# Multiplying forty quads of the first stage in fp32r halves, rounded by ScalarE, with the rests made by GpSimd

## The chip, the cores and the metric

The kernel runs on one core of one Trainium2 chip. The metric is the device time of one execution in microseconds: the median of three runs. Beside it stands one execution taken by the hardware profiler, from which all times of instructions come.

## The reference

The function takes x (8192 x 128) and a sparse but densely stored matrix A (8192 x 8192, some 256 MB in fp32) with positive entries and a full diagonal:

```
def lap_mul(A, x):
    d = 1 / sqrt(sum(A, axis=-1))
    return d[:, None] * (A @ (d[:, None] * x))
z  = leaky_relu(lap_mul(A, x) @ W1 + b1, 0.1)
d2 = sq[:, None] + sq[None, :] - 2 z @ z.T          # sq = sum(z*z, -1)
S  = exp(-sqrt(max(d2, 0) + 1e-10) / 2)             # only the 4 largest of a row are kept
out = lap_mul(S + A, x) @ W2 + b2
return layernorm(x + out)
```

For this case the first `lap_mul` matters: the sums of A's rows, x scaled by them (`xs`), and the product of A with `xs`.

## The kernel before

A is stored transposed and cut into 16 x 16 blocks of 512 x 512. A block, called a quad, is one load of 1 MB onto 128 partitions x 2048 fp32 numbers (four tiles of 128 x 512). Quad (b, q) belongs to row block b and column block q.

The **first stage** streams all 256 quads once, row block by row block (`one`, loaded by SyncE, SP, at L673). VectorE adds the quads of a row block (`add_quad`, L1489, 15 adds, then `add_tiles`, L1494 and L1495), TensorE sums the result over the partitions (`row_sums`, L782, with a column of ones), VectorE copies the sums (`read_sums`, L1499), ScalarE takes a square root (L1052), and VectorE refines its reciprocal and scales x (`scale_xs`, L1507), which gives `xs` for column block b. As soon as `xs` of column block q is there, quad (b, q) can be multiplied while it still lies in its slot: `product` (L773), four fp32 products of 128x128 by 128x512 that accumulate in the PSUM bank of row b. A profile shows each fp32 product as two records, so a quad has eight. Row block b multiplies its quads with q < b when they arrive, and (b, b) after its own scaling, early in the next row; 158 of the 256 quads are multiplied here. When a row block is closed, ScalarE saves its bank (L1063).

A quad lies in one of 18 slots of 1 MB: in `ring`, in `cache` (the place of zh and zl of a later stage) and in parts of R1 and R2. `plan_ab` fixes the order of loads and products, and `next_slot` fixes the slot of each load from the estimate `left` of when a quad is done with. SP waits before a load until the quad that held the slot is added and, if it is multiplied here, multiplied.

Each engine works through its own list in program order. VectorE's list for row b is: the first add (which needs two quads), `read_sums(b - 1)`, the second add, `scale_xs(b - 1)`, the remaining adds, `add_tiles(b)`. TensorE's list is the products of the row, then `row_sums`.

The **second stage** loads the other 98 quads again (`two`) and multiplies them in fp32r halves: ScalarE rounds a quad to fp32r (`round_2`, L1045, two buffers `ah`), VectorE subtracts to get the rest (`rest_2`, L1572, `al`), and TensorE makes three products for each tile: high xs by high quad (L836), low xs by high quad (L837), high xs by rest (L840), twelve in all. The halves of `xs` are made near the end of the first stage, in the last row block: high ones by ScalarE (`high_half`, L1037), low ones by VectorE (`low_half`, L1513).

Behind that come the scores and the search for the four nearest (TensorE, ScalarE, VectorE's MAX8 and FIND_INDEX8), during which GpSimd makes rests for a third pass over A (`rest_of_piece`, L1305), and a tail, in which GpSimd makes two rests of whole quads (L1448) and VectorE the others. GpSimd does nothing in the first stage; its first work are casts of 128x128 (L1278, L1279) in the second.

Of the kernel before, what the change touches and what calls it, by code (L numbers as in the profile page):

```python
# [6 lines left out]
F32 = mybir.dt.float32  # L7
# [8 lines left out]
BC = 512  # L16
# [11 lines left out]
SLOTS_END = (0, 1, 2, 3, SLOTS_2, SLOTS_2 + B // TB)  # L28
# [4 lines left out]
YB = 7  # L33
SUMS_EARLY = 2
STEP_2 = 3
LOW_AT = 10
# [50 lines left out]
def plan_ab():  # L87

    loads, products, closed = [], [], {}
    for b in range(B):  # L90
        keep = [q for q in range(b + 1, B) if b in held(q)]
        low = list(range(b))
        high = [q for q in range(b + 1, B) if q not in keep]
        order = []
        while low or high:
            more_high = len(high) * (len(order) + 1) > 0 and len(high) >= len(low)
            order.append((high if more_high else low).pop(0))
        order += keep[::-1] + [b]
# [31 lines left out]
def build(nc, x, at, W1, b1, W2, b2, consts, out, xs_dram, xh_dram, xl_dram, acc_dram):  # L130
# [7 lines left out]
    closed = {b: max(prod_at[bq] for bq in flat if bq[0] == b) for b in range(B)}  # L138


    def left(n):
        b, q = one[n]
        if (b, q) not in prod_at:
            return n + 2
        return n + 3 if q < b else B * (q + 1) + AHEAD + 4

    n_slots = SLOTS_A + SLOTS_X + len(SLOTS_Y)
# [14 lines left out]
    for n in range(n_one + len(two)):  # L162
        if n < n_one - STREAM_END:
            k = next_slot(n, [*range(SLOTS_A), *(k for k, b in SLOTS_Y.items() if left(n) <= B * (b + 1)),
                              *(k for k, b in X_FROM.items() if left(n) <= B * b)])
# [13 lines left out]
    with ctx:  # L179
# [44 lines left out]
        slots_a += [R2[:, b * BC:b * BC + SLOT].rearrange("p (k c) -> p k c", c=BC) for b in SLOTS_Y.values()]  # L224
        total = R1[:, N + 2 * SLOT:N + 3 * SLOT]
# [119 lines left out]
        xl_ok = sem("xl_ok")  # L345
        rnd_2 = sem("rnd_2")
# [105 lines left out]
        halves = range(min(q for r, q in two), B)  # L452
# [200 lines left out]
        def _(sp):  # L653
# [8 lines left out]
            for n, (b, q) in enumerate(one + two):  # L662
                m = before_of[n]
                if m is not None and m >= n_one:
                    sp.wait_ge(al_ok, m - n_one + 1)
                elif n >= n_one and slot_of[n] in X_FROM:
                    sp.wait_ge(prod1, len(flat))
                    sp.wait_ge(xl_ok, len(halves))
                elif m is not None:
# [90 lines left out]
        def _(pe):  # L760
# [3 lines left out]
            def product(b, q):  # L764
                n = load_at[b, q]
                first = started[b] == 0
                started[b] += 1
                pe.wait_ge(ld_a[slot_of[n]], turn_of[n])
                pe.wait_ge(xs_ok, q + 1)
                if first and b >= YB:  # L770
                    pe.wait_ge(y_saved, b - YB + 1)
                for k in range(TB):
                    i = pe.matmul(PS[:, b % YB], xs[:, q * TB + k], slots_a[slot_of[n]][:, k],  # L773
                                  start=first and k == 0, stop=prod_at[b, q] == closed[b] and k == TB - 1)
# [51 lines left out]
            for n, (b, q) in enumerate(two):  # L826
# [6 lines left out]
                pe.wait_ge(xl_ok, q - halves[0] + 1)  # L833
# [194 lines left out]
        def _(act):  # L1028
# [10 lines left out]
            def round_2(n):  # L1039
                act.wait_ge(ld_a[slot_of[n_one + n]], turn_of[n_one + n])  # L1040
                if n < 2:
                    free_of_stage_1(act, SLOTS_B + n)
                else:
                    act.wait_ge(prod2, n - 1)
                act.activation(ah_2[n % 2][:, :, :], slots_a[slot_of[n_one + n]], ACT.Copy).then_inc(rnd_2, 1)  # L1045

            for b in range(B):
                if b == B - 1:
                    for q in halves[:-2]:
                        high_half(q)  # L1050
                act.wait_ge(sums_read, b + 1)
                act.activation(tiny[:, 0, 0:TB], rowsum[:, b * TB:(b + 1) * TB], ACT.Sqrt).then_inc(root_ok, 1)  # L1052
                if b == B - 1:
# [3 lines left out]
                    round_2(1)  # L1057
                while saved < B and all(q <= b for r, q in flat if r == saved):
# [6 lines left out]
                    saved += 1  # L1065
                if b < B - 1:
# [205 lines left out]
        def _(pool):  # L1272
# [161 lines left out]

            pool.wait_ge(z2_ok, 2 + GT // TB)
# [35 lines left out]
        def _(v):  # L1471
# [44 lines left out]
            for b in range(B):  # L1516
                for i in range(1, B):
# [5 lines left out]
                    if b == B - 1:  # L1523
                        for k, q in enumerate(halves[:-2]):
                            if i == LOW_AT + k // 2:
                                low_half(q)
                add_tiles(b)

            read_sums(B - 1)
# [36 lines left out]
            def rest_2(n):  # L1566
                v.wait_ge(rnd_2, n + 1)
                if n < 2:
                    v.wait_ge(prod1, max(prod_at[r, q] for r, q in flat if q // TB == n))
# [210 lines left out]
```

## Time and profile before

| | us |
|---|---|
| median of 3 runs | 2683.36 |
| lowest and highest run | 2681.94, 2683.89 |
| profiled execution, its time | 2679.84 |
| profiled execution, span from first to last instruction | 2678.0 |
| TensorE busy | 2456.8 |
| VectorE busy | 2319.3 |
| ScalarE busy | 1606.8 |
| GpSimd busy | 1193.2 |
| first stage: last row sums on TensorE at | 708.07 |
| second stage: first product at | 718.86 |

The span has stages with different limits, so the totals say little about the first one. The profile can be cut into stretches, with the busy time of each engine in each; there a full stretch of TensorE is one in which every microsecond saved or added on TensorE counts. The order in time of one engine gives the price of one instruction and the idle time ahead of it, with what ended it.

### The profile page before, as it was taken

To read this page: it belongs to the slowest core of one execution; us is meant where nothing else is said; L and a number is where in the kernel's file an instruction comes from. 1 tells how busy PE (TensorE), PEld (TensorE's weight loads), DVE (VectorE), ACT (ScalarE), POOL (GpSimd) and SP (SyncE) were. 2 spreads that over 40 slices of the span, in tenths; PEclk is the share of its full clock that TensorE was granted. 3 is DMA by queue.
4 is the path that set the end of the run, shared out by engine and by line. 5 is a ranking of instruction groups with operands and counts; after the bars stand their busy time and mean duration, and the time that the engine had idled before them with its cause. 6 is when DMAs were issued, how large, how long until landed. Compare 5 with 4: busy or idle time off the path is not lost.

```text
span 2678.0 us, 29073 instructions
## 1 busy us (share of the span) xinstructions
PE 2456.8 (92%) x9356; PEld 1710.4 (64%) x9356; DVE 2319.3 (87%) x1411; ACT 1606.8 (60%) x1905; POOL 1193.2 (45%) x987
## 2 busy tenths in 40 slices
PE   0467999999999999899999999999999998899998
PEld 0133444444577777577778787877878775577776
DVE  7998889976788887999999999989999877488887
ACT  0000000000377776899998989889898876477776
POOL 0000000000000000067788888878787895777772
PEclk9678999999999999999999999999999999999999
DMA  9999999997699981035565555545555568999996
GB/s 383 421 405 402 399 421 421 421 421 291 236 374 345 341 329 52 0 114 170 147 170 147 168 149 141 175 135 177 146 173 148 168 179 320 398 400 402 400 402 244
DMA packets 147948, 718.58 MB, mean 268 GB/s; under 512 B 19024, under 2 KB 26960, under 8 KB 86608
## 3 DMA queue, kind: packets, MB, share of 16 engines
q1 hardware_dynamic: 124384, 670.49, 66.7%
q0 software_dynamic: 18800, 37.77, 5.7%
q10 hardware_dynamic: 4608, 8.39, 0.8%
q8 instruction: 79, 1.29, 0.2%
q14 instruction: 77, 0.63, 0.1%
HBM read 680.40 MB, written 36.18 MB: 268 GB/s over the span
## 4 chain that ended last, share of the span: by engine, by line
PE 59%; DMA 9%; issue 9%; DVE 9%; ACT 9%; POOL 3%; SPq 0%; ACTq 0%; POOLq 0%; DVEq 0%
PE PS L773 19%; PE PS L872 5%; PE PS L874 5%; PE PS L873 5%; DMA ring<-at 4%; ACT R L1147 3%; PE PS L840 3%; DMA R<-at 3%; PE PS L916 3%; PE PS L917 3%; PE PS L927 3%; PE PS L836 2%; PE PS L837 2%; PE PS L977 2%; DVE R L1629 2%
## 5 line engine op out<-in xcount | busy, mean ns | idle before, releaser
L1305 POOL TENSOR_TENSOR al<-ring,ah 128x1024 fp32r<-128x1024 f32 x264 | 643.7, 2439 | 181.6 <-ACT ah L1118 168.0
L1629 DVE MAX8 R<-R 128x8 f32<-128x8192 f32 x64 | 555.8, 8685 | 68.6 <-ACT R L1147 68.4
L1147 ACT ACTIVATE R<-PS 128x1024 f32<-128x1024 f32 x512 | 518.0, 1018 | 112.0 <-PE PS L880 82.6
L1632 DVE FIND_INDEX8 R<-R,R 128x8 uint32<-128x8192 f32 x64 | 555.9, 8685 | 0.3 <-issue 0.3
L1278 POOL CAST zst<-zh 128x128 fp32r<-128x128 f32 (+1 forms) x64 | 26.3, 411 | 1112.8 <-DVE zl L1564 811.1
L872 PE MATMUL PS<-zh,zst 128*128 128x512 f32 x1024 | 407.2, 398 | 28.5 <-ACT PS L1133 12.7
L874 PE MATMUL PS<-zh,zst 128*128 128x512 f32 x1024 | 400.4, 391 | 0.0
L873 PE MATMUL PS<-zl,zst 128*128 128x512 f32 x1024 | 400.2, 391 | 0.0
L1133 ACT ACTIVATE PS<-R 128x1024 f32<-128x1024 f32 x310 | 318.0, 1026 | 6.6
L1052 ACT ACTIVATE tiny<-rowsum 128x4 f32<-128x4 f32 x16 | 3.3, 205 | 482.1 <-DVE rowsum L1499 482.1
L773 PE MATMUL PS<-cache,R 128*128 128x512 f32 x584 | 263.5, 603 | 16.7 <-DMA cache<-at 11.3
L1489 DVE TENSOR_TENSOR R<-R,cache 128x2048 f32<-128x2048 f32 x106 | 242.9, 2292 | 19.8 <-DMA cache<-at 17.5
L872 PEld LDWEIGHTS PS<-zh,zst 128*128 128x128 f32 x1024 | 192.2, 188 | 96.9 <-ACT PS L1133 25.0
L1464 POOL DMA_INDIRECT R<-xs_dram,R x176 | 192.5, 1094 | 61.4 <-issue 52.7
L874 PEld LDWEIGHTS PS<-zh,zst 128*128 128x128 f32 x1024 | 192.3, 188 | 41.6
L873 PEld LDWEIGHTS PS<-zl,zst 128*128 128x128 f32 x1024 | 192.3, 188 | 39.8 <-issue 0.7
L773 PEld LDWEIGHTS PS<-cache,R 128*128 128x128 f32 x584 | 112.3, 194 | 157.6 <-issue 144.7
L773 PE MATMUL PS<-ring,R 128*128 128x512 f32 x384 | 175.9, 605 | 11.9 <-DMA ring<-at 6.4
L1572 DVE TENSOR_TENSOR al<-ring,ah 128x2048 fp32r<-128x2048 f32 x66 | 151.0, 2290 | 35.5 <-ACT ah L1045 33.0
L1489 DVE TENSOR_TENSOR R<-R,ring 128x2048 f32<-128x2048 f32 x72 | 165.0, 2291 | 11.6 <-DMA ring<-at 9.6
L987 PE MATMUL PS<-ah_t,xsh 128*128 128x512 f32 x368 | 153.3, 417 | 11.8 <-ACT ah_t L1197 11.6
L1045 ACT ACTIVATE ah<-ring 128x2048 fp32r<-128x2048 f32 x66 | 126.4, 1915 | 62.7 <-PE PS L840 59.9
(181 smaller groups left out, 4515.5 us busy)
## 6 DMA issues: line engine op xcount, KB each, us to landing
R<-at SPq DMA_DIRECT2D x160, 1024.0 KB, 14.7
ring<-at SPq DMA_DIRECT2D x148, 1024.0 KB, 9.4
ring<-at SPq DMA_DIRECT2D x264, 512.0 KB, 3.8
cache<-at SPq DMA_DIRECT2D x117, 1024.0 KB, 20.3
acc_dram<-R POOLq DMA_DIRECT2D x78, 256.0 KB, 5.7
raw_sq<-at SPq DMA_DIRECT2D x18, 1024.0 KB, 14.4
raw_z<-at SPq DMA_DIRECT2D x18, 1024.0 KB, 15.3
raw_ring<-at SPq DMA_DIRECT2D x17, 1024.0 KB
```

The source lines that it names most:

```text
L773: i = pe.matmul(PS[:, b % YB], xs[:, q * TB + k], slots_a[slot_of[n]][:, k], start=first and k == 0, stop=prod_at[b, q] == closed[b] and k ...
L872: pe.matmul(bank, zst[:, par, 0], zh[:, cols], start=not on_seed, stop=False, skip_group_check=True)
L873: pe.matmul(bank, zst[:, par, 0], zl[:, cols], start=False, stop=False, skip_group_check=True)
L874: i = pe.matmul(bank, zst[:, par, 1], zh[:, cols], start=False, stop=on_seed, skip_group_check=True)
L987: pe.matmul(bank, xsh[:, t], ah_t[n % HIGH_T][:, k], start=from_zero and k == 0, stop=False, skip_group_check=True)
L1133: act.activation(pair(False, 0, c), sq_row[c], ACT.Copy).then_inc(seeded, 1)
L1147: act.activation(score[j % 2][:, c * EC:(c + 1) * EC].rearrange("p (b c) -> p b c", b=2), pair(first, j, c), ACT.Copy).then_inc(copied, 1)
L1305: pool.tensor_tensor(al[:, k % SPLIT], raw[k % RAW], ah[:, k % SPLIT].bitcast(F32), ALU.subtract)\
L1464: pool.indirect_dma_start(gx[f % GX][:, j, m], None, xs_dram, bass.IndirectOffsetOnAxis(ap=sidx[:, FIN[f] * TB + j, m:m + 1], axis=0))\
L1489: v.tensor_tensor(total.rearrange("p (k c) -> p k c", c=BC), other, slots_a[slot_of[n]], ALU.add)\
L1629: v.max(top[:, j], score[j % 2]).then_inc(dve3, 1)
L1632: v.max_index(place[:, j], top[:, j], score[j % 2]).then_inc(placed, 1)
```

## The change

In row blocks 11 to 15 (`SPLIT_FROM`) the quads of column blocks 0 to 7 (`SPLIT_Q`), forty in all, are no longer multiplied as fp32. ScalarE rounds such a quad into one of the two `ah` buffers (`round_1`), GpSimd writes the rest, the raw quad less the rounded one, over the raw quad (`rest_1`), after VectorE has added it, and TensorE makes the twelve fp32r products. The other quads of these rows stay as they are. The order of loads in these rows now alternates between split and plain quads. The halves of `xs` for columns 0 to 7 are made earlier, in row block 10, the high ones by ScalarE (`early_high`) and the low ones by GpSimd (`early_low`). The slots change with that: the `ah` buffers and the early halves lie where slots were, these are not used any more from row 10 or 11 on, and two new ones (`SLOTS_W`) lie over `xs` of columns 0 to 7, which nobody reads in fp32 after row 10. VectorE's low halves of the other columns move behind all adds of the last row.

```
+SPLIT_FROM, SPLIT_Q = 11, 2 * TB
+SOON = 3
...
+        if b >= SPLIT_FROM:
+            plain_q = [q for q in range(SPLIT_Q, B) if q != b]
+            order = [q for both in zip(range(SPLIT_Q), plain_q) for q in both]
+            order += range(len(plain_q), SPLIT_Q)
...
-        halves = range(min(q for r, q in two), B)
+        halves = range(SPLIT_Q, B)
...
+                if (b, q) in split_at:
+                    m = split_at[b, q]
+                    bank = PS[:, b % YB]
+                    pe.wait_ge(xl_early, q + 1)
+                    pe.wait_ge(rnd_1, m + 1)
+                    for k in range(TB):
+                        pe.matmul(bank, half_of_xs(0, q)[:, k], ah_2[m % 2][:, k], start=first and k == 0, stop=False,
+                                  skip_group_check=True)
+                        pe.matmul(bank, half_of_xs(1, q)[:, k], ah_2[m % 2][:, k], start=False, stop=False,
+                                  skip_group_check=True)
+                    pe.wait_ge(low_1, m + 1)
+                    for k in range(TB):
+                        i = pe.matmul(bank, half_of_xs(0, q)[:, k], low_of_slot[slot_of[n]][:, k], start=False,
+                                      stop=False, skip_group_check=True)
+                    i.then_inc(prod1, 1)
+                    return
...
+            def round_1(m):
+                n = load_at[split1[m]]
+                act.wait_ge(ld_a[slot_of[n]], turn_of[n])
+                if m < 2:
+                    free_of_stage_1(act, SLOTS_B + m)
+                else:
+                    act.wait_ge(prod1, prod_at[split1[m - 2]])
+                act.activation(ah_2[m % 2][:, :, :], slots_a[slot_of[n]], ACT.Copy).then_inc(rnd_1, 1)
+
             for b in range(B):
-                if b == B - 1:
-                    for q in halves[:-2]:
-                        high_half(q)
+                if b == SPLIT_FROM - 1:
+                    for q in range(SPLIT_Q):
+                        early_high(q)
                 act.wait_ge(sums_read, b + 1)
                 act.activation(tiny[:, 0, 0:TB], rowsum[:, b * TB:(b + 1) * TB], ACT.Sqrt).then_inc(root_ok, 1)
...
+                row_split = [m for m, (r, q) in enumerate(split1) if r == b + 1]
+                for m in row_split[:SOON]:
+                    round_1(m)
...
+                for i, m in enumerate(row_split[SOON:]):
+                    round_1(m)
...
+            def rest_1(m):
+                n = load_at[split1[m]]
+                pool.wait_ge(rows_added, (B - 1) * (n // B) + max(n % B, 1))
+                hold(pool)
+                pool.wait_ge(rnd_1, m + 1)
+                hold(pool)
+                pool.tensor_tensor(low_of_slot[slot_of[n]][:, :, :], slots_a[slot_of[n]],
+                                   ah_2[m % 2][:, :, :].bitcast(F32), ALU.subtract).then_inc(low_1, 1)
+
+            for q in range(SPLIT_Q):
+                early_low(q)
+            for m in range(len(split1)):
+                rest_1(m)
...
+            for q in halves[:-2]:
+                low_half(q)
             read_sums(B - 1)
             scale_xs(B - 1)
```

On ScalarE, at the end of the first stage, the list of before has a square root for each row block (R_50 is R2, where a closed bank is saved), and then the high halves and the first roundings of the second stage:

```order
L1052 ACTIVATE tiny<-rowsum 128x4
L1063 ACTIVATE R_50<-PS 128x512
L1037 ACTIVATE xsh<-R_49 128x512 x9
L1052 ACTIVATE tiny<-rowsum 128x4
L1045 ACTIVATE ah_81<-ring 128x2048
```

Between two square roots now stand eight roundings; this is the beginning of row block 12, where `ah_91` and `ah_92` are the two buffers:

```order
L1119 ACTIVATE tiny<-rowsum 128x4
L1112 ACTIVATE ah_91<-R_49 128x2048
L1112 ACTIVATE ah_92<-R_49 128x2048
L1112 ACTIVATE ah_91<-cache 128x2048
L1133 ACTIVATE R_50<-PS 128x512
L1112 ACTIVATE ah_92<-cache 128x2048
```

Three roundings of the next row stand behind the square root, then the save of the closed bank, then the other five. On TensorE, row block 12 of before begins behind the row sums of row 11 with plain fp32 products, four a quad:

```order
L782 MATMUL PS<-ones,R_49 128x1 x4
L773 MATMUL PS<-ring,R_49 128x512 x4
L773 MATMUL PS<-R_49 128x512 x4
L773 MATMUL PS<-cache,R_49 128x512 x20
L773 MATMUL PS<-ring,R_49 128x512 x4
```

Now the first quad is a split one, from the last pair of its products with the rounded half on; `low_80` is the rest that GpSimd has written over the slot:

```order
L811 MATMUL PS<-ah_91,xsh 128x512
L813 MATMUL PS<-ah_91,xsl 128x512
L817 MATMUL PS<-low_80,xsh 128x512 x4
L824 MATMUL PS<-ring,R_49 128x512 x4
L811 MATMUL PS<-ah_92,xsh 128x512
L813 MATMUL PS<-ah_92,xsl 128x512
```

Four products with the rest (L817) stand between the products with the rounded half (L811, L813) and the next plain quad (L824), so TensorE passes them only when GpSimd is done with that quad.

## Rows read from the trace of the kernel before

**Rows 1.** Busy time by stretch, row blocks 10 to 15: length, then engines, clock, DMA.

```profile
core 0: us, PE busy (x) PEld busy (x) DVE busy (x) ACT busy (x) POOL busy (x), PEclk, DMA share, GB/s
432.29:470.95 38.66, 38.66 (x99) 17.61 (x98) 36.37 (x24) 0.80 (x2) 0.00 (x0) 1.00 1.01 421
470.95:513.04 42.09, 42.09 (x106) 19.13 (x106) 39.08 (x25) 0.80 (x2) 0.00 (x0) 1.00 1.01 420
513.04:558.57 45.53, 45.53 (x115) 20.66 (x114) 37.73 (x24) 0.80 (x2) 0.00 (x0) 1.00 1.02 421
558.57:607.53 48.96, 48.96 (x123) 22.17 (x122) 37.64 (x24) 0.80 (x2) 0.00 (x0) 1.00 1.01 421
607.53:659.92 52.39, 52.39 (x130) 23.69 (x130) 37.63 (x24) 0.80 (x2) 0.00 (x0) 1.00 0.84 327
659.92:718.86 58.94, 58.94 (x146) 26.65 (x146) 48.05 (x43) 10.43 (x16) 0.00 (x0) 1.00 0.54 192
```

**Rows 2.** TensorE in order of time: start, length, line, operands, count.

```profile
603.28 3.60 PE L773 MATMUL PS<-R 128*128 128x512 f32 x8
606.72 0.95 PE L782 MATMUL PS<-ones,R 128*128 128x1 f32 x8
...
722.00 0.39 PE L836 MATMUL PS<-ah,xsh 128*128 128x512 f32 x1
...
723.81 1.07 PE L840 MATMUL PS<-al,xsh 128*128 128x512 f32 x4
724.72 0.39 PE L836 MATMUL PS<-ah,xsh 128*128 128x512 f32 x1
```

**Rows 3.** SP's waits from 400 to 760: us in total, times, longest.

```profile
SPq L672 <- PE PS L773: 201.6, 57, 13.8
```

**Rows 4.** VectorE in order of time, rows 14 and 15, idle time in brackets.

```profile
607.70 0.16 DVE L1499 COPY rowsum<-PS 128x4 f32<-128x4 f32 x1 [10.56 <-PE PS L782]
...
687.82 1.29 DVE L1513 TENSOR_TENSOR xsl<-R,xsh 128x512 fp32r<-128x512 f32 x2
...
709.06 0.16 DVE L1499 COPY rowsum<-PS 128x4 f32<-128x4 f32 x1 [1.86 <-PE PS L782]
...
710.68 0.69 DVE L1507 TENSOR_TENSOR R<-R,dsc 128x512 f32<-128x512 f32 x1
```

**Rows 5.** GpSimd's subtractions: ns min/median/max of a line; one in time.

```profile
L1448 POOL TENSOR_TENSOR al_t<-R,ah_t x2: 4562/4565/4568, 2243.7 to 2248.2; 128x2048 fp32r<-128x2048 f32 x2
...
L1305 POOL TENSOR_TENSOR al<-ring,ah x264: 2373/2410/2700, 1146.4 to 2235.7; 128x1024 fp32r<-128x1024 f32 x132
...
1142.33 1.30 POOL L1389 TENSOR_TENSOR xgl<-R,xgh 128x512 fp32r<-128x512 f32 x1
```

**Rows 6.** ScalarE in order of time: a square root; a rounding of the second stage.

```profile
607.96 0.21 ACT L1052 ACTIVATE tiny<-rowsum 128x4 f32<-128x4 f32 x1 [31.34 <-DVE rowsum L1499]
...
731.42 1.92 ACT L1045 ACTIVATE ah<-ring 128x2048 fp32r<-128x2048 f32 x1 [1.65 <-DMA ring<-at]
```

**Rows 7.** VectorE, then GpSimd, in order of time, 811 to 817 us.

```profile
811.32 2.29 DVE L1572 TENSOR_TENSOR al<-R,ah 128x2048 fp32r<-128x2048 f32 x1
814.07 2.31 DVE L1572 TENSOR_TENSOR al<-R,ah 128x2048 fp32r<-128x2048 f32 x1 [0.46 <-ACT ah L1045]
...
811.53 2.23 POOL L1278 CAST zst<-zh 128x128 fp32r<-128x128 f32 x1 [811.08 <-DVE zl L1564]
813.72 0.28 POOL L1279 CAST zst<-zl 128x128 fp32r<-128x128 f32 x1
813.95 0.29 POOL L1278 CAST zst<-zh 128x128 fp32r<-128x128 f32 x1
814.19 2.35 POOL L1279 CAST zst<-zl 128x128 fp32r<-128x128 f32 x1
```

**Rows 8.** The page's group of VectorE's search: busy, mean ns, idle before.

```profile
L1629 DVE MAX8 R<-R 128x8 f32<-128x8192 f32 x64 | 555.8, 8685 | 68.6 <-ACT R L1147 68.4
```

**Rows 9.** TensorE early in the first stage, with the idle time ahead.

```profile
119.66 3.70 PE L773 MATMUL PS<-ring,R 128*128 128x512 f32 x8 [1.94 <-DMA ring<-at]
...
269.15 5.32 PE L773 MATMUL PS<-ring,R 128*128 128x512 f32 x8 [4.50 <-DMA ring<-at]
```

More of the change, by code:

```diff
@@ L97, in plan_ab @@
             order.append((high if more_high else low).pop(0))
+        if b >= SPLIT_FROM:
+            plain_q = [q for q in range(SPLIT_Q, B) if q != b]
+            order = [q for both in zip(range(SPLIT_Q), plain_q) for q in both]
+            order += range(len(plain_q), SPLIT_Q)
+            assert not keep
         order += keep[::-1] + [b]
@@ L138, in build @@
     closed = {b: max(prod_at[bq] for bq in flat if bq[0] == b) for b in range(B)}
+    split1 = [(b, q) for b in range(SPLIT_FROM, B) for q in loads[b] if q < SPLIT_Q]
+    assert split1 == sorted(split1, key=lambda bq: prod_at[bq])
+    split_at = {bq: m for m, bq in enumerate(split1)}
     def left(n):
@@ L163, in build @@
         if n < n_one - STREAM_END:
-            k = next_slot(n, [*range(SLOTS_A), *(k for k, b in SLOTS_Y.items() if left(n) <= B * (b + 1)),
+            k = next_slot(n, [*(k for k in range(SLOTS_A)
+                                if k not in SLOTS_SPLIT or left(n) <= B * SLOTS_SPLIT[k] + TB),
+                              *(k for k in SLOTS_W if n >= B * SPLIT_FROM + TB),
+                              *(k for k, b in SLOTS_Y.items() if left(n) <= B * (b + 1)),
                               *(k for k, b in X_FROM.items() if left(n) <= B * b)])
@@ L224, in build @@
         slots_a += [R2[:, b * BC:b * BC + SLOT].rearrange("p (k c) -> p k c", c=BC) for b in SLOTS_Y.values()]
+        slots_a += [R1[:, k * SLOT:(k + 1) * SLOT].rearrange("p (k c) -> p k c", c=BC) for k in range(len(SLOTS_W))]
+        slot_top = [top_of["ring"] + k * SLOT * 4 for k in range(SLOTS_B)]
+        slot_top += [top_of["R1"] + (N + k * SLOT) * 4 for k in range(2)]
+        slot_top += [top_of["zh"] + k * SLOT * 4 for k in range(SLOTS_A - SLOTS_2)]
+        slot_top += [top_of["R1"] + k * SLOT * 4 for k in (2, 3)]
+        slot_top += [top_of["R2"] + b * BC * 4 for b in SLOTS_Y.values()]
+        slot_top += [top_of["R1"] + k * SLOT * 4 for k in range(len(SLOTS_W))]
+        low_of_slot = {k: sb(f"low_{k}", [P, TB, BC], F32R, at=slot_top[k])
+                       for k in sorted({slot_of[load_at[bq]] for bq in split1})}
         total = R1[:, N + 2 * SLOT:N + 3 * SLOT]
@@ L451, in build @@
         ends = list(itertools.accumulate(sum(r == b for r, q in two) for b in blocks2))
-        halves = range(min(q for r, q in two), B)
+        assert min(q for r, q in two) < SPLIT_Q
+        halves = range(SPLIT_Q, B)
         last_quad = {}
@@ L668, in _ @@
                     sp.wait_ge(xl_ok, len(halves))
+                elif m is None and slot_of[n] in SLOTS_W:
+                    k = SLOTS_W.index(slot_of[n])
+                    sp.wait_ge(xl_early, (k + 1) * TB)
+                    sp.wait_ge(prod1, max(prod_at[r, q] for r, q in flat if r < SPLIT_FROM and q // TB == k))
                 elif m is not None:
@@ L767, in product @@
                 started[b] += 1
+                if first and b >= YB:
+                    pe.wait_ge(y_saved, b - YB + 1)
+                if (b, q) in split_at:
+                    m = split_at[b, q]
[13 more added lines that the diff above has]
+                    return
                 pe.wait_ge(ld_a[slot_of[n]], turn_of[n])
                 pe.wait_ge(xs_ok, q + 1)
-                if first and b >= YB:
-                    pe.wait_ge(y_saved, b - YB + 1)
                 for k in range(TB):
                     i = pe.matmul(PS[:, b % YB], xs[:, q * TB + k], slots_a[slot_of[n]][:, k],
-                                  start=first and k == 0, stop=prod_at[b, q] == closed[b] and k == TB - 1)
+                                  start=first and k == 0, stop=prod_at[b, q] == closed[b] and k == TB - 1,
+                                  skip_group_check=b >= SPLIT_FROM)
                 i.then_inc(prod1, 1)
@@ L832, in _ @@
                     pe.wait_ge(y_ok, blocks2.index(row_of_bank[b]) + 1)
-                pe.wait_ge(xl_ok, q - halves[0] + 1)
+                if q in halves:
+                    pe.wait_ge(xl_ok, q - halves[0] + 1)
                 pe.wait_ge(rnd_2, n + 1)
@@ L1065, in _ @@
                     saved += 1
+                for i, m in enumerate(row_split[SOON:]):
+                    round_1(m)
+                    if b == B - 2 and i >= 1:
+                        for q in halves[2 * (i - 1):min(2 * i, len(halves) - 2)]:
+                            high_half(q)
                 if b < B - 1:
@@ L1568, in rest_2 @@
                 if n < 2:
-                    v.wait_ge(prod1, max(prod_at[r, q] for r, q in flat if q // TB == n))
+                    free_of_stage_1(v, SLOTS_W[n])
                 else:
```

30 lines of the change are left out of this document (22 added, 8 removed).

## The prediction

> **What bounds the kernel now.** I read the busy time by stretches first, cut at the ends of the row sums of successive row blocks. In row blocks 10 to 15 TensorE is busy for the whole of every stretch at the full granted clock, GpSimd is not used at all, ScalarE hardly, and VectorE is busy for 37.6 to 37.7 us in each of rows 12 to 14, whatever the row's length [rows 1]. So the row lengths, 42.09, 45.53, 48.96, 52.39 and 58.94 us for rows 11 to 15, are TensorE's. Its order in time gives the prices: one fp32 quad takes 606.72 - 603.28 = 3.44 us, the four row-sum products 607.53 - 606.72 = 0.81 us, and one quad of the second stage, which is already multiplied in fp32r halves, 724.72 - 722.00 = 2.72 us, of which the last four products, those of the rest, are 724.72 - 723.81 = 0.91 and the first eight 1.81 [rows 2]. That nothing else limits these rows shows on SP's queue: it waited 201.6 us for products that hold slots [rows 3]. A microsecond won or lost here moves everything behind it, since TensorE goes straight from this stage into the next.
>
> VectorE has a second role. Its first add of a row runs early, but before the second it waits for the row sums of the row before (10.56 us at 607.70) [rows 4]; so of a row's adds all but the first lie between two row sums, and 37.6 us is what such a row costs it.
>
> **The change, part by part.**
>
> TensorE. Forty quads (8 in each of rows 11 to 15) go from 3.44 to 2.72 us: 40 x 0.72 = 28.8 us removed, all of it on the path. This is the gain that everything else is set against.
>
> GpSimd. Forty rests of 128x2048 are new. The trace has two passes of exactly this shape, 4.565 us each, and the half-size ones at 2.41 agree [rows 5]. That is 8 x 4.565 = 36.5 us a row, on an engine that was idle. Eight low halves of xs (128x512, 1.30 us each [rows 5]) are added in row 10.
>
> ScalarE. Forty roundings of 1.92 us [rows 6], 15.4 us a row: cheap, but their place matters. ScalarE rounds the first quad of row b+1 only after its square root of row b, which starts 607.96 - 607.53 = 0.43 us after TensorE has ended the row sums [rows 1, 6]. TensorE's next product is that quad. So it waits 0.43 + some 0.1 + 1.92 + some 0.15 for the hand-over = 2.6 us, does its first eight products until 4.4, and waits again for GpSimd's rest, which can begin at 2.6 and is there at 2.6 + 4.57 + 0.15 = 7.3: 2.9 us more. Each row begins with 5.5 us of waiting where there was none. Queued behind TensorE's wait are all products of the row, so no other work covers it. Two rounding buffers also mean that quad m is rounded only when quad m-2 is multiplied, so GpSimd never gets more than about one quad ahead.
>
> The end of a row. Where a plain product lies between two split ones, the pair takes 3.44 + 2.72 = 6.2 us and GpSimd's 4.57 fits. Behind the last plain one the split quads follow one another at GpSimd's pace, 1.85 us slower than TensorE's. Following quad by quad with these prices gives waits of 6.8 us in row 11 (1.4 + 3 x 1.8), 4.2 in row 12, 2.4 in row 13 and none in rows 14 and 15.
>
> Without any further cost the rows then change by -8 x 0.72 + 5.5 + tail: +6.5, +3.9, +2.1, -0.3, -0.3, together +12 us, and about 1 us more where the last loads wait for slots that split quads hold longer. The saving is eaten by the rows' beginnings and ends alone.
>
> VectorE beside GpSimd. The change lets GpSimd read two SBUF operands while VectorE adds two SBUF operands, which the first stage never did before. The trace has two encounters of this kind. VectorE's subtraction of two SBUF tiles ran from 811.32 to 813.61; a GpSimd cast that started inside it, at 811.53, took 2.23 us and ended at 813.76. The next two casts fell in VectorE's gap and took 0.28 and 0.29. The fourth started at 814.19 inside VectorE's next subtraction (814.07 to 816.38) and took 2.35 [rows 7]. A cast of 0.28 us that lasts until 0.15 us behind VectorE's end was held off for the whole instruction. Against MAX8, with one SBUF input, GpSimd's passes run at 2.41 us [rows 5, 8]. So the two share something that a two-input instruction of VectorE keeps to itself. What no row shows is the other direction, a GpSimd pass of 4.57 us that starts first. Bounds: nothing (both overlap, +12 us as above) or full serial work. I take full serial work, because the encounters in rows 7 are the nearest there are, both of them, and GpSimd's gain from being stopped would be the same sum anyway: if GpSimd is stopped for each add, its 36.5 us still have to be found between 37.6 us of VectorE.
>
> The Trainium skill, in "SBUF — State Buffer", section "Who interferes with whom", says that a VectorE instruction with two SBUF inputs contends with a GpSimd instruction that reads SBUF, and that whichever starts first keeps the shared pair for its whole length. The casts of rows 7 agree for the side that the trace shows. By this rule the sum is the serial one; without it, the +12 us above.
>
> The sum. A row on the shared resource: 37.6 + 36.5 = 74.1 us; up to 16 hand-overs of 0.15 add 2.4; I take 76. Adds, rests and products of a row cannot slide into another row, since adds wait for row sums, row sums for all products of the row, and those for the last rest. Rows 11 to 14: 4 x 76 - (42.09 + 45.53 + 48.96 + 52.39) = +115.0. Row 15: 76 less the 2.3 of a next row's first add, then on VectorE the low halves, now all behind the adds (six at 0.645 = 3.9 us), then 711.37 - 709.06 = 2.3 until xs is scaled [rows 4], then the last product, 3.44: 83.3 against 58.94, +24.4. Row 10: VectorE has 36.4 of 38.66 us to do [rows 1] and eight passes of 1.30 are put among them: 46.8, +8.1. Together +147.5 us. The profiled execution took 2679.84 us; 2827.3. The median of the runs shown is 3.5 us above it: **2831**. The next stages keep their length: their loads, roundings and rests are the same, and GpSimd is done by then.
>
> **The rivals.**
>
> A, no sharing loss (the two long casts had another cause): +13 us, 2697. For: each of the four engines has time. Against: rows 7, where two casts of four on the same line differ by eight times and only by what VectorE ran.
>
> B, faster: GpSimd's pass is short and nothing contends. The mechanism is the wait at the rows' beginnings and ends, which shrinks with the pass. At VectorE's 2.29 us the beginning costs 2.6 + 0.6, the tail nothing, and a row is worth -5.8 + 3.2 = -2.6: -13 us, 2670. It decides at about 3.6 us per pass, where the waits equal 28.8. Against: 4.565 us twice in [rows 5]. ScalarE's late start remains in any case.
>
> C, GpSimd holds the shared resource for half of its pass: a row is 37.6 + 18.3 and hand-overs, 57: rows 11 to 14 +39, row 15 +5, row 10 +3: +47, 2731. No row speaks for or against.
>
> D, VectorE wins every encounter as long as it has an add queued: GpSimd's first rest then starts at about 37.6, the first quad ends at 43, and the remaining 41 us of the row follow as in the case without contention: 84 a row, 8.4 more than the forecast in each of five, 2873. Rows 7 don't decide it, since VectorE had gaps there. To this side belongs TensorE's clock: after an idle time of 1.94 us eight products took 3.70, but after 4.50 us 5.32 [rows 9]; the new waits lie between and beyond. TensorE then has slack in most of the row, so I count a few microseconds at most.
>
> **How the numbers follow.** Forecast 0.62, C 0.12, A 0.13, D 0.07, B 0.06. Forecast, C and D hold 0.81, so the range goes from C's side, 2715, to just beyond D, 2880. About 0.2% is what a measurement can tell from no change here, 5.4 us. A is 13 us slower, with an uncertainty of about as much, so a sixth of it ends faster and a sixth within 0.2%. Faster: 0.06 + 0.02 = 0.08. Same: 0.02 from A and as much from B, 0.04. Slower: 0.88.
>
> **What would show it.** Right: GpSimd's passes in rows 11 to 15 well above 4.57 us, or VectorE's adds well above 2.29, in sum some 30 us a row; row sums 76 us apart; TensorE waiting for the rests in every row, its granted clock below 1 in places; and the second stage as long as before. Wrong: passes at 4.57 beside adds at 2.29, rows of 48 to 52 us and waits at the rows' beginnings alone (A), or rows shorter than before (B).

## The result and the profile after

The changed kernel takes 2816.7 us (median of 4 runs, 2816.41 to 2817.93) against 2682.69 before (median of 4): a ratio of 1.05, 95% interval 1.0483 to 1.0517. It is slower by 134 us; the forecast was 2831 and slower. The profiled execution took 2816.41 us, its span is 2814.6.

The stretches of after, cut at the ends of the row sums of successive row blocks as in [rows 1], are these (length, busy time of each engine with its count, granted clock of TensorE, DMA share, GB/s); the five lines are row blocks 11 to 15:

```profile
core 0: us, PE busy (x) PEld busy (x) DVE busy (x) ACT busy (x) POOL busy (x), PEclk, DMA share, GB/s
476.84:549.02 72.18, 50.03 (x137) 32.43 (x138) 71.42 (x25) 15.78 (x10) 47.63 (x8) 0.78 0.75 297
549.02:621.24 72.22, 50.52 (x145) 31.73 (x146) 71.46 (x25) 15.77 (x10) 47.29 (x8) 0.81 0.58 218
621.24:693.52 72.28, 51.88 (x153) 32.07 (x154) 71.52 (x25) 15.77 (x10) 47.73 (x8) 0.85 0.61 236
693.52:765.76 72.24, 57.42 (x161) 34.41 (x162) 71.48 (x25) 15.77 (x10) 47.71 (x8) 0.83 0.57 222
765.76:850.14 84.38, 64.06 (x181) 37.61 (x182) 79.37 (x40) 21.93 (x20) 47.74 (x8) 0.83 0.39 147
```

Three things are to be seen against [rows 1]. The full engine is now VectorE (71.5 of 72.2 us), not TensorE. A row's length no longer depends on how many quads it multiplies: four rows of 72.2 us where there were 42.09 to 52.39. And VectorE's count is the same 25 or so instructions as before, in 71.5 instead of 37.6 us, so it does the same work and is held 33.8 us a row. Rows 11 to 14 are together 288.92 - 188.97 = 99.95 us longer, row 15 84.38 - 58.94 = 25.4, row 10 44.80 - 38.66 = 6.1: 131.5 us. The second stage's first product moved by just that, from 718.86 to 850.14, and that stage itself is as long as before: from the first of its rest products to the last are 290.6 us, before 290.5. The other 5 us between the two profiled spans (2814.6 and 2678.0) lie behind it, spread over the later stages.

Where VectorE is held shows in the order in time, first VectorE, then GpSimd, from the middle of row block 12 (start, length, line, operands, count, idle time ahead in brackets):

```profile
576.43 2.29 DVE L1585 TENSOR_TENSOR R<-R,R 128x2048 f32<-128x2048 f32 x1
578.75 6.52 DVE L1585 TENSOR_TENSOR R<-R,cache 128x2048 f32<-128x2048 f32 x1
...
577.05 6.08 POOL L1524 TENSOR_TENSOR low<-cache,ah 128x2048 fp32r<-128x2048 f32 x1 [2.81 <-DVE R L1585]
```

GpSimd's pass starts at 577.05, inside VectorE's add, waits for that add's end at 578.72 and ends at 583.13, 4.41 us behind it. VectorE's next add starts at 578.75 and ends at 585.27, 2.14 us after the pass is over, so all but some 0.15 of its 2.29 us lie behind the pass. From 578.72 to 585.27 are 6.55 us for one pass and one add, which alone take 4.565 [rows 5] and 2.29 [rows 7]: 6.86. The two engines alternate, with 0.3 us of overlap at the ends. The add after the held one runs free, the next one is held by the next pass, and so on. GpSimd's 40 passes, by the slot that they read (ns: least, median, most; first and last start):

```profile
L1524 POOL TENSOR_TENSOR low<-ring,ah x17: 4544/6439/6467, 485.0 to 820.0; 128x2048 fp32r<-128x2048 f32 x17
L1524 POOL TENSOR_TENSOR low<-cache,ah x14: 4547/6405/6467, 480.5 to 769.4; 128x2048 fp32r<-128x2048 f32 x14
L1524 POOL TENSOR_TENSOR low<-R,ah x9: 4548/6430/6475, 495.6 to 828.9; 128x2048 fp32r<-128x2048 f32 x9
```

Medians of 6.4 us are one pass plus the wait for the add in progress; the least, 4.55, is the price alone. Even an instruction of four numbers is held if it has two SBUF inputs. The two operations of the Newton step on the reciprocal of row 11's sums, at the start of row 12, took 0.16 us each before; now they read:

```profile
552.74 4.46 DVE L469 TENSOR_TENSOR tiny<-tiny 128x4 f32<-128x4 f32 x1
557.24 4.48 DVE L470 TENSOR_TENSOR tiny<-tiny,rowsum 128x4 f32<-128x4 f32 x1
...
552.64 9.06 POOL L1524 TENSOR_TENSOR low<-R,ah 128x2048 fp32r<-128x2048 f32 x2 [6.36 <-DVE R L1585]
```

TensorE's list, which had no wait in these rows, now waits for the rests, for the row sums' last add and for the first rounding of a row (us in total, times, longest), and GpSimd itself mostly for VectorE's adds:

```profile
POOL low L1524 <- DVE R L1585: 116.7, 34, 6.4
PE PS L817 <- POOL low L1524: 77.1, 32, 5.8
PE PS L834 <- DVE R L1591: 15.4, 2, 9.4
PE PS L811 <- ACT ah L1112: 12.9, 5, 2.6
```

The first quad behind the row sums of row 12 answers to [rows 2]; the products with the rounded quad stand 0.43 us apart, not 0.23, until the clock is back:

```profile
620.43 1.81 PE L834 MATMUL PS<-ones,R 128*128 128x1 f32 x8
624.83 0.76 PE L811 MATMUL PS<-ah,xsh 128*128 128x512 f32 x1 [2.59 <-ACT ah L1112]
625.39 0.63 PE L813 MATMUL PS<-ah,xsl 128*128 128x512 f32 x1
625.82 0.63 PE L811 MATMUL PS<-ah,xsh 128*128 128x512 f32 x1
...
629.48 1.21 PE L817 MATMUL PS<-low,xsh 128*128 128x512 f32 x4 [1.20 <-POOL low L1524]
```

### The profile page after: what moved, and what is told of

It is laid out like the page before. It is cut to its first block, busy times and chain, and to the rows that moved or that the text cites. A ratio compares the mean times of both kernels' runs of the same rounds, so it can differ in the third digit from the quotient of the medians.

```text
span 2814.6 us, 29616 instructions
## 1 busy us (share of the span) xinstructions
PE 2490.7 (88%) x9516; PEld 1771.2 (63%) x9516; DVE 2494.0 (89%) x1408; ACT 1683.8 (60%) x1950; POOL 1462.3 (52%) x1035
## 4 chain that ended last, share of the span: by engine, by line
PE 46%; DVE 22%; ACT 9%; issue 9%; DMA 9%; POOL 4%; SPq 0%; ACTq 0%; POOLq 0%; DVEq 0%
DVE R L1585 12%; PE PS L824 8%; PE PS L925 5%; PE PS L927 5%; PE PS L926 5%; DMA ring<-at 4%; ACT R L1222 4%; DMA R<-at 3%; PE PS L969 3%; PE PS L893 3%; PE PS L980 3%; PE PS L970 3%; PE PS L889 2%; PE PS L890 2%; PE PS L1030 2%
## 5 line engine op out<-in xcount | busy, mean ns | idle before, releaser
L1585 DVE TENSOR_TENSOR R<-R,cache 128x2048 f32<-128x2048 f32 x91 | 249.3, 2740 | 16.9 <-DMA cache<-at 14.9
L1515 POOL TENSOR_TENSOR xsl<-R,xsh 128x512 fp32r<-128x512 f32 x8 | 24.4, 3086 | 450.6 <-ACT xsh L1103 450.6
L1585 DVE TENSOR_TENSOR R<-R,ring 128x2048 f32<-128x2048 f32 x80 | 235.8, 2947 | 6.5 <-DMA ring<-at 4.3
L927 PEld LDWEIGHTS PS<-zh,zst 128*128 128x128 f32 x1024 | 192.8, 188 | 41.8
L824 PE MATMUL PS<-cache,R 128*128 128x512 f32 x352 | 161.7, 610 | 17.3 <-DMA cache<-at 11.9
L1769 DVE TENSOR_TENSOR al_t<-R,ah_t 128x1024 fp32r<-128x1024 f32 x102 | 120.3, 1221 | 48.3 <-ACT ah_t L1272 48.2
```

Source lines behind the costliest of these rows:

```text
L927: i = pe.matmul(bank, zst[:, par, 1], zh[:, cols], start=False, stop=on_seed, skip_group_check=True)
L1585: v.tensor_tensor(total.rearrange("p (k c) -> p k c", c=BC), other, slots_a[slot_of[n]], ALU.add)\
```

## The experiments

The theory is the prediction's: a GpSimd pass that reads two SBUF operands and a VectorE instruction that does the same run one after the other, and a row is their sum. The rivals are that the rests are slow by themselves and TensorE waits for them whatever VectorE does, that GpSimd's writes or its memory traffic as such slow VectorE, and that the fine cut of the work is at fault. Eleven kernels tell these apart; each was timed beside runs of the kernel before (medians 2681.48 to 2684.61).

### VectorE with one input, the passes as they are

```
+if b >= SPLIT_FROM and i > 1:
+    v.max(tiny[:, 4], slots_a[slot_of[n]]).then_inc(rows_added, 1)
+    return
+if b >= SPLIT_FROM:
+    other = total.rearrange("p (k c) -> p k c", c=BC)
```

> The changed kernel, but in row blocks 11 to 15 VectorE's adds from the second on are replaced by a search of the eight largest numbers over the same quad: one SBUF input of 128x2048 where the add has two, and nearly the same length. It leaves out those adds, so the row sums of these rows are not A's; everything else, every wait too, is as in the changed kernel. Theory (a two-input instruction of VectorE and a reading pass of GpSimd keep each other out): GpSimd's rests fall from a median of 6.4 us to 4.55 beside VectorE's one-input instructions, the rows from 72.2 us to what the waits at their beginnings and ends give: 48.8, 49.5, 51.1, 52.2 us for rows 11 to 14; with 6 us from row 10, about +19 us against before, 2702 us. Rival (GpSimd's passes are slow beside other traffic, or the handshakes cost the time): rests stay above 6 us, rows near 72, time near 2817.

Measured: 2720.2 us, ratio 1.0142 (1.0122 to 1.0163), so 96.5 us of the 134 vanish although GpSimd does the same forty passes. Its passes are back at their own price (least, median, most in ns):

```profile
L1524 POOL TENSOR_TENSOR low<-ring,ah x17: 4523/4567/5532, 487.5 to 731.1; 128x2048 fp32r<-128x2048 f32 x17
```

VectorE's searches beside them from 480 to 700 us (busy, mean ns, idle before), and rows 11 and 12 as stretches:

```profile
L1586 DVE MAX8 tiny<-ring 128x8 f32<-128x2048 f32 x21 | 48.2, 2295 | 0.6
```

```profile
479.90:531.77 51.87, 41.90 (x139) 27.07 (x139) 51.10 (x25) 15.79 (x10) 37.28 (x8) 0.89 0.96 391
531.77:582.99 51.22, 44.13 (x146) 28.55 (x145) 50.46 (x25) 15.78 (x10) 37.35 (x8) 0.90 0.80 322
```

Passes of 4.567 us and searches of 2.295 us run beside each other as if alone. Rows 13 and 14 took 52.0 and 52.8. The total was put at 2702 and missed by 18 us: rows 11 to 14 are 3.1, 1.7, 0.9 and 0.6 us longer than written down, and row 15, for which nothing was counted, 10.6 us longer than before. VectorE is full here too, 51.1 of 51.87 us, and the reason is the few instructions that still have two inputs; in order of time, VectorE and then GpSimd:

```profile
535.06 4.48 DVE L469 TENSOR_TENSOR tiny<-tiny 128x4 f32<-128x4 f32 x1
539.57 4.47 DVE L470 TENSOR_TENSOR tiny<-tiny,rowsum 128x4 f32<-128x4 f32 x1
...
534.97 9.05 POOL L1524 TENSOR_TENSOR low<-R,ah 128x2048 fp32r<-128x2048 f32 x2 [5.10 <-DVE tiny L1586]
```

Two operations on four numbers cost 8.6 us of a row. They also settle what the search leaves open: it has one input less than an add, but it writes only eight numbers too. These operations write next to nothing and are held all the same, so a second input is enough. This run, too, does not show the rows free of the conflict.

### GpSimd that only writes, or reads once

```
-pool.tensor_tensor(low_of_slot[..], slots_a[..], ah_2[m % 2][..].bitcast(F32), ALU.subtract)
+pool.memset(low_of_slot[..].bitcast(F32), 0.0)          # e2_write_only
+pool.tensor_copy(low_of_slot[..], ah_2[m % 2][..].bitcast(F32))   # e7_one_read
```

> The changed kernel, but GpSimd fills the slot with zeros instead of subtracting: it writes the same 128x2048 numbers and reads nothing. It leaves out the rests. Theory (what is shared is a way of reading): VectorE's adds stay at 2.29 us, GpSimd's fills are all of one short length, and a row changes by 8 x 0.72 us less and a wait of some 2.6 us for the first rounding more, about -3 us each; with +6 from row 10 about 2674 us. Rival (the two engines keep each other out whatever GpSimd does): adds are lengthened by a fill's length eight times a row, and rows 11 to 13 grow with it.

> The changed kernel, but GpSimd copies the rounded quad over the slot instead of subtracting: one SBUF input instead of two. It leaves out the rests. A copy of 128x1024 took 1.05 us in the trace of before, so 2.1 us is the estimate for one of 128x2048. Theory (any reading pass counts): eight times a row VectorE is held up for nearly the length of a copy, a row of VectorE is 37.6 + 8 x 1.9 = 53 us, rows 11 to 14 about 53 each, +23 us, row 15 some +8, row 10 +6: about 2720 us. Rival (only two-input passes of GpSimd collide): adds at 2.29 us, rows as in the write-only run, about 2674 us.

Measured: filling 2689.56 us, ratio 1.003 (1.0019 to 1.0042); copying 2714.51, 1.0121 (1.0101 to 1.0141). First the fills and the copies (least, median, most in ns), then a group of adds beside the fills and one beside the copies, both from 480 to 700 us (busy, mean ns, idle before):

```profile
L1524 POOL MEMSET low<- x40: 1804/1811/1822, 481.0 to 708.0; 128x2048 f32 x40
```

```profile
L1524 POOL CAST low<-ah x40: 1889/3490/3951, 481.1 to 729.9; 128x2048 fp32r<-128x2048 f32 x40
```

```profile
L1584 DVE TENSOR_TENSOR R<-R,ring 128x2048 f32<-128x2048 f32 x29 | 66.5, 2292 | 9.7 <-DMA ring<-at 9.0
```

```profile
L1584 DVE TENSOR_TENSOR R<-R,ring 128x2048 f32<-128x2048 f32 x25 | 71.4, 2857 | 0.7
```

The fills are all alike within 1% and the adds stay at 2.292 us: what GpSimd writes does not collide with a two-input add. A pass with one input already does: the copies are stretched from 1.89 us to a median of 3.49 and the adds to 2.857, and rows 11 to 13 are 51.0 us each. VectorE is busy for 50.3 of them against 37.7, so each copy of 1.89 us holds it for some 1.6. The conflict is about reading, and its price goes with the length of the GpSimd pass: a shorter one holds VectorE for less. The copies came within 6 us of the 2720 written down. The fills missed their 2674 by 15.6 us; their rows (41.8, 44.1, 47.5 and 51.0 us for rows 11 to 14) are those of the next run, which shows why. (Fills did hold one instruction, which is told at the end.)

### No rests at all

```
-pe.wait_ge(low_1, m + 1)
-    i = pe.matmul(bank, half_of_xs(0, q)[:, k], low_of_slot[slot_of[n]][:, k], start=False,
+    i = pe.matmul(bank, half_of_xs(0, q)[:, k], ah_2[m % 2][:, k], start=False,
...
-for m in range(len(split1)):
-    rest_1(m)
```

> The changed kernel without GpSimd's forty rests: TensorE multiplies the rounded quad a third time in the rest's place, and waits for no rest. It leaves out the rests; ScalarE's roundings, the slots and GpSimd's eight early low halves stay. This is the most that the change could give with the rests for nothing. Theory: the saving of 0.72 us per quad is there, and each row still begins with a wait of 2.6 us for the first rounding: 5 x (-5.8 + 2.6) = -16, row 10 +6: about 2673 us. Rival (the slots or the loads limit the last rows, or ScalarE's roundings do): rows 11 to 15 not shorter than before, 2690 us or more.

Measured: 2689.46 us, ratio 1.0029 (1.0016 to 1.0041). This run missed too, by 16 us: with rests that cost nothing the kernel should have won, and it still loses 7.8 us. Rows 11 to 14 became 41.58, 44.07, 47.50 and 50.97 us, 0.5 less than before in row 11 and some 1.4 in each of the others, where 8 x 0.72 less the 2.6 us start are 3.2. The start of row 12 shows the rest of it:

```profile
517.66 0.95 PE L833 MATMUL PS<-ones,R 128*128 128x1 f32 x8
521.05 0.51 PE L811 MATMUL PS<-ah,xsh 128*128 128x512 f32 x1 [2.44 <-ACT ah L1111]
521.36 0.62 PE L813 MATMUL PS<-ah,xsl 128*128 128x512 f32 x1
521.78 0.63 PE L811 MATMUL PS<-ah,xsh 128*128 128x512 f32 x1
...
524.34 1.29 PE L816 MATMUL PS<-ah,xsh 128*128 128x512 f32 x4
525.47 3.59 PE L823 MATMUL PS<-ring,R 128*128 128x512 f32 x8
```

and the row as one stretch:

```profile
518.47:562.54 44.07, 41.63 (x146) 27.71 (x145) 37.74 (x24) 15.78 (x10) 0.00 (x0) 0.96 0.99 396
```

After the row sums and an idle time of 2.44 us the products stand 0.425 us apart from the second on (521.36 to 521.78), the pace of 1.2 GHz, against 0.227 in the second stage [rows 2]: this first quad takes 525.47 - 521.05 = 4.42 us instead of 2.72, and the granted clock of the row is 0.96. Here a wait of 2.4 us costs 4.1. On top come row 10, 6.1 us longer, and row 15, 3.5 us longer, in which VectorE waited 8.3 us for a late load.

### The plain quad first

The run before with one edit more: each pair begins with its plain quad, so that ScalarE's rounding runs under 3.44 us of products.

```
-order = [q for both in zip(range(SPLIT_Q), plain_q) for q in both]
+order = [q for both in zip(plain_q, range(SPLIT_Q)) for q in both]
```

> The run without rests, with one edit: in rows 11 to 15 the pairs of loads and products begin with the plain quad, so that TensorE has 3.44 us of work while ScalarE makes the first rounding. It leaves out the rests, as that run does. Theory (a row loses 2.5 us to the wait for the first rounding and 1.7 us more because the nine or so products behind the wait run at the lower clock): no wait and no slow products at the rows' beginnings; rows 12 to 14 another 4.2 us shorter, 39.9, 43.3, 46.8 us, row 11 held by VectorE's 37.7 at about 38.5; in sum some 15 to 19 us less than the run without rests, 2672 us. Rival (the loads or VectorE limit these rows once the rests are gone): less than 8 us gained.

Measured: 2670.18 us, ratio 0.9953 (0.9936 to 0.997), some 19 us less than without the edit. TensorE waits for no rounding, and rows 12 to 14 have the lengths written down, 39.9, 43.3 and 46.8 (row 11 took 40.3, not 38.5), with TensorE full at the full clock:

```profile
516.40:556.27 39.87, 39.87 (x146) 26.50 (x146) 37.73 (x24) 15.79 (x10) 0.00 (x0) 1.00 1.01 421
556.27:599.59 43.32, 43.32 (x154) 28.02 (x154) 37.73 (x24) 15.86 (x10) 0.00 (x0) 1.00 1.01 417
599.59:646.36 46.77, 46.77 (x163) 29.55 (x162) 37.74 (x24) 15.76 (x10) 0.00 (x0) 1.00 0.94 380
```

Each is 5.6 to 5.7 us below [rows 1], the 8 x 0.72 of the sum. In these rows the start wait with its clock was the whole difference, 4.2 us each.

### The same passes in halves, fewer rows

```
+for ks in (slice(0, TB // 2), slice(TB // 2, TB)):                # e5_half_passes
+    i = pool.tensor_tensor(low_of_slot[..][:, ks], slots_a[..][:, ks], ah_2[m % 2][:, ks].bitcast(F32), ALU.subtract)
...
-SPLIT_FROM, SPLIT_Q = 11, 2 * TB                                  # e6_from_13
+SPLIT_FROM, SPLIT_Q = 13, 2 * TB
```

> The changed kernel with each rest cut into two GpSimd passes of 128x1024. Theory (the sum counts): VectorE is held up twice as often for half as long, a row stays at 72 us within 2, the time within 10 us of 2817. Rival (it is the length of one GpSimd instruction that hurts, because a waiting short instruction of VectorE sits behind all of it): rows fall by 5 us or more.

> The changed kernel with rows 13 to 15 split instead of rows 11 to 15. Theory: a split row takes 72.2 us whatever its number, since VectorE's and GpSimd's work in it is the same: row 13 +23, row 14 +20, row 15 +25; the early halves now fall into row 12, where VectorE has 8 us to spare, and cost nothing: +68 us, 2750 us. Rival (cost in proportion to the quads, 134 x 24 / 40): +80 us, 2763 us.

Measured: halves 2813.06 us, 1.0489 (1.047 to 1.0508); from row 13 on 2751.67, 1.026 (1.0241 to 1.0279). With halves the two engines take turns in smaller steps; VectorE, then GpSimd:

```profile
572.93 4.32 DVE L1587 TENSOR_TENSOR R<-R,R 128x2048 f32<-128x2048 f32 x1
577.28 4.33 DVE L1587 TENSOR_TENSOR R<-R,cache 128x2048 f32<-128x2048 f32 x1
...
570.71 21.86 POOL L1525 TENSOR_TENSOR low<-cache,ah 128x1024 fp32r<-128x1024 f32 x5
```

Now every add is held for half a pass instead of every second one for a whole pass, 4.3 and 4.3 in place of 2.29 and 6.52, and rows are 71.4 to 72.1 us long. The sum counts, not the cut. From row 13 on, rows 13 to 15 to their sums take 71.49, 72.30 and 72.26 us while rows 11 and 12 are as before (42.09, 45.53): 68 us to the start of the second stage, which grows with the number of rows and says that the cost belongs to each row by itself. Row 12 there also makes the eight early low halves and is not longer, since VectorE has 45.53 - 37.7 = 7.8 us to spare in it, where row 10 has 2.3 [rows 1].

### The rests by VectorE

```
-for m in range(len(split1)):      # GpSimd's list
-    rest_1(m)
...
+if b >= SPLIT_FROM and i % 2 == 1 and i > 1:      # VectorE's, behind its adds; the last one behind the tiles
+    rest_1(SPLIT_Q * (b - SPLIT_FROM) + i // 2 - 1)
```

> The changed kernel with its forty rests made by VectorE, each behind the add of the quad after it, and none by GpSimd. Theory (rests and adds are one sum, whoever makes the rests, and VectorE's 2.29 us per rest is cheaper than the 4.23 us for which GpSimd holds it up): a row of VectorE is 37.6 + 8 x 2.29 = 56 us; rows 11 to 14 +35 us, row 15 about +6, row 10 +6: +47 us, 2730 us. Rival (the order and the waits of the split quads cost the rows, not the sum): rows stay near 72 us, or fall to the 42 to 51 us of the run without rests.

Measured: 2752.65 us, ratio 1.0264 (1.0245 to 1.0283). If the two engines cannot read at once, the engine that needs 2.28 us for a rest should do it, not the one that holds the other for 4.2; this is 64 us better than the change. Rows 11 to 14 take 57.1, 55.9, 57.0 and 55.5 us, as written down (56). The total was forecast 23 us lower and missed for the most part in row 15, which takes 71.9 to its sums; there VectorE waited for loads, SP's queue for products that hold the slots, and TensorE for VectorE's rests, 16.2 of its 41.7 us of rows 11 to 15 (us in total, times, longest):

```profile
DVE R L1574 <- DMA ring<-at: 10.0, 3, 9.7
DVE R L1574 <- DMA R<-at: 9.9, 2, 5.7
...
SPq L707 <- PE PS L824: 81.8, 8, 25.6
PE PS L817 <- DVE low L1605: 41.7, 14, 4.2
```

The three wait in a circle: a rest stands behind an add that needs a load, the products of the plain quads (L824), for which SP waits, stand in TensorE's list behind the products with the rests, and the load waits for a slot. The forecast of this run left that out; no run here shows which of the three sets the length.

### Only as many rests as VectorE has time for

Eleven quads (columns 5 to 7 of row 13, 4 to 7 of rows 14 and 15), each behind plain ones in the row's order, with VectorE making the rest behind an add and a single slot over `xs`. Two variants followed: that slot used from row 14 on only, and rows 14 and 15 alone.

```
+SPLIT_OF = {13: (5, 6, 7), 14: (4, 5, 6, 7), 15: (4, 5, 6, 7)}
+for k, q in enumerate(SPLIT_OF[b]):
+    order.insert(3 + 3 * k, q)
...
+    if b >= SPLIT_FROM and i in (4, 7, 10, 13)[:len(SPLIT_OF[b])]:
+        rest_1(split_at[b, SPLIT_OF[b][i // 3 - 1]])
...
-    *(k for k in SLOTS_W if n >= B * SPLIT_FROM + 2 * TB),
+    *(k for k in SLOTS_W if n >= B * (SPLIT_FROM + 1)),          # e9_late_slot
...
-SPLIT_OF = {13: (5, 6, 7), 14: (4, 5, 6, 7), 15: (4, 5, 6, 7)}
+SPLIT_OF = {14: (4, 5, 6, 7), 15: (4, 5, 6, 7)}                  # e10_rows_14
```

> A version that is meant to gain: 3 quads of row 13 and 4 each of rows 14 and 15 (columns 5 to 7, 4 to 7) are split, their rests are made by VectorE, which has time to spare in these rows, each row begins with three plain products so that the first rounding is done in time, and GpSimd makes only four early low halves, in row 12. Theory: 11 x 0.72 = 7.9 us saved where VectorE's 37.6 + 2.29 per rest stays below TensorE's row; row 13 44.5 against 46.8, row 14 46.8 against 49.5, row 15 at the limit: about -7 us, 2676 us. Rival (fewer slots or late loads in row 15 eat it, as in the run without rests): within 3 us of before.

> The version with 11 split quads again, but the slot over xs of columns 4 to 7 takes loads from row 14 on, not within row 13, where its first load had to wait for a plain product of the same row and all loads behind it on SP's queue with it: VectorE waited 8.5 us for a quad there and row 13 took 54.0 us instead of 46.8. Theory: row 13 falls to about 47 us, rows 14 and 15 stay at 49.6 and some 57 us: 7 us less than the version before it, -7 us against the kernel before, 2675 us. Rival (fewer slots make another load late in the same row): within 3 us of the kernel before.

> The same with rows 14 and 15 alone, 8 quads. Theory: 8 x 0.72 = 5.8 us less on TensorE, of which row 15 keeps 2.2 and row 14 2.8 as in the version with 11 quads: -5 us, 2677 us. Rival: late loads in row 14, whose slots are now freed one row later: within 2 us of before.

Measured: 2681.16 us, ratio 0.9996 (0.9987 to 1.0005); with the late slot **2675.19**, 0.9973 (0.9964 to 0.9982); rows 14 and 15 alone 2678.11, 0.9987 (0.9978 to 0.9996). The first lost its gain in row 13, which took 54.0 us: SP waited for the plain products that read the `xs` under the slot (L704, with all later loads queued behind it), VectorE for a load, and TensorE for VectorE's rest:

```profile
SPq L704 <- PE PS L825: 27.3, 1, 27.3
...
DVE R L1575 <- DMA R<-at: 9.1, 4, 8.5
...
PE PS L818 <- DVE low L1606: 2.9, 1, 2.9
```

With the slot opened later the wait is gone, and so is the loss; rows 13 and 14 of that run:

```profile
559.80:606.68 46.88, 46.88 (x135) 24.37 (x134) 43.96 (x27) 6.31 (x5) 0.00 (x0) 1.00 0.94 375
606.68:656.27 49.59, 49.59 (x147) 26.61 (x146) 46.08 (x28) 8.23 (x6) 0.00 (x0) 1.00 0.91 358
```

48.96 and 52.39 were there [rows 1]; three and four times 0.72 are 2.2 and 2.9, measured 2.1 and 2.8. TensorE stays full at the full clock because VectorE, with 44.0 and 46.1 us, stays below the row's length. This version is faster than both kernels, by 0.27% over the kernel before; without row 13 it loses 2.9 us again.

## Why the prediction was right, point by point

**The mechanism** was right and is shown: with the same passes and one-input instructions on VectorE 96.5 of the 134 us go, with no rests 127. That a pass that starts first holds VectorE, the direction that no row of before showed and that the forecast took from the bound of full serial work, stands in the trace of after at 578.75 (6.52 instead of 2.29 us). The Trainium skill, in "SBUF — State Buffer", section "Who interferes with whom", gave the same rule, and these rows agree with it for both sides.

**The row, mis-sized.** The step "37.6 + 36.5 + 2.4 of hand-overs, I take 76" came out as 72.2 us. The hand-overs have the wrong sign: the ends overlap. A pass and an add back to back take 6.55 us, not 6.86 plus 0.3, and VectorE's busy time rises by 33.8 us a row, 4.2 for each of eight passes of 4.565. Four rows of 3.8 us are the 15 us between 115.0 and 99.95, and nearly the whole of the 14 us by which the forecast was too long.

**Row 10** was put at +8.1 and came to +6.1 for the same reason. The low halves and the adds alternate there too:

```profile
451.00 24.43 POOL L1515 TENSOR_TENSOR xsl<-R,xsh 128x512 fp32r<-128x512 f32 x8 [450.55 <-ACT xsh L1103]
...
455.78 3.24 DVE L1585 TENSOR_TENSOR R<-R,ring 128x2048 f32<-128x2048 f32 x1
```

An add is held 0.95 us by a pass of 1.30. **Row 15**, +24.4 forecast and +25.4 measured, holds two errors that cancel, which is luck: the forecast is too long by 2.3 up to the row sums' start (73.7 forecast, 837.16 - 765.76 = 71.4 measured), and too short behind it: VectorE's low halves, the scaling and one quad were counted, 9.6 us, but TensorE still had three quads to multiply, the first at the lower clock, and took 850.14 - 837.16 = 13.0.

**The saving** of 0.72 us a quad was right; the runs with the plain quad first and with eleven quads show it to 0.1 us. In the changed kernel nothing of it reaches the end, since TensorE isn't the bound.

**The row's start** was sized too low in one term. The wait itself, 2.6 us forecast, is 2.59 in row 13. But the clock, counted as "a few microseconds at most" because TensorE would have slack, costs 1.7 us more behind the wait in rows 12 to 14 of the run without rests. In the changed kernel the slack hides it, as the prediction said; where the rests are taken away nothing does, and the starts are most of the 19 us between the runs with the split and with the plain quad first (4.2 us in each of rows 12 to 14, 3.2 in row 15, 1.3 in row 11). The prediction's +12 us for a change without contention was not met by any run as such: none has rests at their own price beside VectorE's own adds.

**The rivals.** A (no sharing, 2697) falls by the run with one-input instructions. B (faster, if the pass is short enough) is not what happened, and its point of decision, 3.6 us a pass, was too kind: with rests of no length in the same order the kernel is still 0.3% slower. C (held for half a pass) falls: 4.2 of 4.565 us. D (VectorE wins every encounter) falls: GpSimd gets in behind the add in progress, as at 577.05, and the medians of 6.4 us say the same of most passes. (Its row of 84 us is 8.0 more than 76, not 8.4.)

## What to carry to other kernels

Before work goes to an idle GpSimd, add the time of its passes that read SBUF to VectorE's two-input time in that stretch: here the sum, less some 0.3 us for each turn, was the length of the stretch, with whole passes and with halves. If VectorE alone would do the work in less time, it should, up to its slack. The first piece of work behind a barrier should be one whose operands are ready: a wait of 2.4 us ahead of TensorE cost 4.1 in three rows here. A slot that a new use holds longer delays loads in the rows behind, so the first version of an edit that gains by the sum may lose it there (2681.16 against 2675.19 us for one slot opened later).

## What was not expected of the hardware

What an idle time does to TensorE's clock differs from row to row. In the run without rests each of rows 12 to 15 begins with the same 0.8 us of row sums and 2.44 us of idle time; the products then fall from 0.227 to 0.425 us each from the second, fourth, fifth and sixth product on. In the run with the rests by VectorE rows 12 to 15 begin with 2.44 to 2.46 us of idle time; in rows 12 and 14 all eight products stand 0.43 us apart, in rows 13 and 15 0.23. So the length of the wait alone doesn't decide it, and what does was not tried.

A fill by GpSimd, which reads nothing, leaves two-input adds alone but holds a one-input instruction on four numbers: in the run with fills the TENSOR_SCALAR of the reciprocal, 0.17 us elsewhere, reads (busy, mean ns, idle before)

```profile
L472 DVE TENSOR_SCALAR tiny<-tiny 128x4 f32<-128x4 f32 x5 | 6.1, 1224 | 0.7
```

that is 1.22 us on average at the starts of rows 11 to 15; in row 12 it starts at 522.33 and ends at 523.58, with the fill that began at 521.75. The two-input operations just ahead of it took 0.16 us each beside the same fill. Which property of that instruction makes it wait for a writer was not tried.
